# Four batches mixed at once in the quarters of the matmul array, with four row buffers

## The chip, the cores and the metric

The kernel runs on one core of a Trainium2 chip. The metric is the time of one execution on the device in microseconds; smaller is better. Several runs of a kernel are given as their median.

## What is computed

A batch of 32 inputs of 64 channels by 1024 positions passes through two layers. Cut to what matters:

```python
# layer 0: grouped convolution + condition, then an FFN with 4-bit weights and low-rank parts
x = x + ffn0(conv(x, cond))
# layer 1: every batch b has a mixing matrix of its own, then one of 8 experts for each row
agg_w = einsum('bk,koi->boi', att, weight)            # att: softmax of a small MLP of cond
agg_b = att @ bias_k
z = einsum('boi,bih->boh', agg_w, x) + agg_b[:, :, None]   # 32 x 64 rows of 1024
logits = z.reshape(2048, 1024) @ gate_w.T + gate_b
selected = argmax(softmax(logits))
x = x + z_row @ expert_w[selected].T + expert_b[selected]
```

The change touches the line that makes `z`, and the logits and the row numbers behind it.

## The kernel before

The 2048 rows (32 batches of 64 channels) lie in SBUF as 16 row tiles `acc[:, t]` of 128 partitions by 1024 FP32 values, 4 KB in each partition. Tile `t` holds batch 2t in partitions 0 to 63 and batch 2t + 1 in partitions 64 to 127. Each engine runs its own program; the programs meet only at semaphores. The matmul unit (TensorE, PE in the profile) writes to eight PSUM banks of 128 x 512 FP32; two banks side by side are a `pair`.

Layer 0 fills some 1065 us and ends when VectorE (DVE) has added the last product to `acc` (semaphore `acc_added`, 352 counts). While its last products run, SyncE (SP) stores the finished rows to DRAM (`x_rows`, line 408), and the mixing matrices are made and written to DRAM (`batch_kernels`, line 481, issued by GpSimd, POOL) and read back (line 486).

The *mixing loop* follows, over the 16 row tiles, with these steps for tile `t`:

- `z_product` (line 1323): the block-diagonal matrix `bdg[:, t]`, 128 x 128 with the two batches' 64 x 64 matrices on its diagonal and zeros elsewhere, times `acc[:, t]`. Two FP32 matmuls of 512 columns, into pair 0 for even tiles and pair 2 for odd ones. A `memset` on GpSimd (line 478) made the zeros.
- `z_bias` (line 718): ScalarE (ACT) adds the mixed bias and writes the 128 x 1024 result to `z32[:, t % 2]`, one of two buffers. It waits for the product, for the store that last read this buffer (`z_stored`), and for the transposes that last read it.
- line 499: GpSimd issues the store of the buffer to DRAM (`z_rows`), from where the expert stage gathers rows later.
- `z_transposed` (line 1331): TensorE turns the buffer in eight 128 x 128 transposes into pair 1.
- `z_copied` (line 989): VectorE copies all of pair 1 into the one SBUF tile `zt`.
- `gate` (line 1339): eight narrow FP32 matmuls, on four strips of 32 columns of the array, give the 8 experts' logits in four parts; `logit` (line 996) adds the gate bias; `pick_out` (line 1346) sums the parts with one small matmul, and `picked` (line 1001) copies the 8 logits of each row to `logits`.

TensorE's order is: transposes of tile t, product of tile t + 2, gate of t, pick of t - 1. VectorE's is: copy of t, logit of t, picked of t - 1. SyncE loads the weights of experts 0 and 1 (`wraw`, line 425, 512 KB each time), one load after each tile's activation.

Then comes routing: VectorE finds each row's expert and slot, a matmul of one-hot matrices gives the table from slots to row numbers (lines 1037 to 1079), and TensorE turns dummy products (`spin`, line 1369) meanwhile. A row number is built from two digits: the lane (`lane`, partition + 1) and the tile number times 128. The expert stage then gathers rows of `z_rows` by that table (line 518), transposes them and multiplies, up to the end.

Of the kernel before, what the change touches and what calls it, by code (L numbers as in the profile page):

```python
# [9 lines left out]
I32 = mybir.dt.int32  # L10
# [35 lines left out]
ONEHOT = 5  # L46
EMPTY = 1 << 20
# [39 lines left out]
def program(nc, x_nat, x_conv, toep, cond_t, ctx_w_t, chan_bias, codes_up, codes_dn, am_up, am_dn, bias_up,  # L87
# [5 lines left out]
    with ctx:  # L93
# [60 lines left out]
        wh = sb(late, "wh", [P, 2, 4, L], F32R)  # L154
        hh = sb(late, "hh", [P, 4, CHUNK], F32R)
# [10 lines left out]
        sb(tail, "gts_too", [P, KT, GQ])  # L166
# [37 lines left out]
        lane = sb(moe, "lane", [P, 1])  # L204
        before = sb(moe, "before", [P, E, E])
# [46 lines left out]
        agg_mm, agg_ready, aggs_stored, bdg_zero = sem("agg_mm"), sem("agg_ready"), sem("aggs_stored"), sem("bdg_zero")  # L252
# [17 lines left out]
        bdg_in = sem("bdg_in")  # L270
# [4 lines left out]
        z_stored = [sem(f"z_stored{i}") for i in range(2)]  # L275
# [30 lines left out]
        def _(sp):  # L306
# [104 lines left out]
            sp.wait_ge(bdg_zero, 1)  # L411
# [27 lines left out]
        def _(pool):  # L439
# [37 lines left out]
            pool.wait_ge(term_ready, NCH * WT)  # L477
            nc.gpsimd.memset(bdg[:], 0.0).then_inc(bdg_zero, 1)
# [11 lines left out]
            nc.gpsimd.iota(lane_i[:], [[1, 1]], base=1, channel_multiplier=1).then_inc(iotas, 1)  # L490
            nc.gpsimd.memset(tri[:], 1.0).then_inc(iotas, 1)
            pool.wait_ge(iotas, 3)
# [3 lines left out]
            for i in rounds(pool, TILES // 2):  # L496
                for k in range(2):
                    wait(pool, z_ready, i * 2 + k + 1)
                    pool.dma_start(z_dram[bass.ds(i * 2 * P + k * P, P)], z32[:, k]).then_inc(z_stored[k], 16)

            for k in range(2):
                pool.wait_ge(z_stored[k], 16 * TILES // 2)
                pool.wait_ge(x_stored[k], 16 * TILES // 2)
# [65 lines left out]
        def _(act):  # L569
# [144 lines left out]
            def z_bias(i, p):  # L714
                act.wait_ge(z_mm, i * 2 + p + 1)
                wait(act, z_stored[p % 2], i * 16 + 16 * (p // 2))
                wait(act, z_tr, i * 2 + p - 1)
                nc.scalar.activation(z32[:, p % 2], pair[2 * (p % 2)][:], ACT.Identity,  # L718
                                     bias=aggb[:, bass.ds(i * 2 + p, 1)]).then_inc(z_ready, 1)

            z_bias(0, 0)
            z_bias(0, 1)
            for i in rounds(act, TILES // 2 - 1):
                for k in range(2):
                    z_bias(i, k + 2)
# [30 lines left out]
        def _(dve):  # L756
            def perceptron(step):
# [15 lines left out]
                else:  # L773
                    dve.wait_ge(aggb_mm, 1)
                    for c in range(2):
                        rows = slice(64 * c, 64 * c + 64)
                        nc.vector.tensor_copy(aggb[rows, :], bank[3][rows, 0:B].rearrange(
                            "p (q c) -> p q c", c=2)[:, :, c]).then_inc(aggb_ready, 1)
# [207 lines left out]
            def z_copied(i, k):  # L986
                dve.wait_ge(z_tr, i * 2 + k + 1)
                wait(dve, gate_mm, i * 2 + k)
                nc.vector.tensor_copy(zt[:], pair[1][:]).then_inc(zt_ready, 1)

            def logit(i, k):
                dve.wait_ge(gate_mm, i * 2 + k + 1)
                dve.sem_inc(dve_passed, 1)

                wait(dve, pick_mm, i * 2 + k - 1)
                nc.vector.tensor_scalar(lt[:, k], bank[6 + k][:, 0:P], gbs[:, 0:1], None, ALU.add).then_inc(lt_ready, 1)

            def picked(i, k):
                dve.wait_ge(pick_mm, i * 2 + k + 1)
                dve.sem_inc(dve_passed, 1)  # L1000
                nc.vector.tensor_copy(logits[:, bass.ds(i * 2 + k, 1)].rearrange("p t e -> p (t e)"),
                                      bank[6 + k][:, P:P + E]).then_inc(logit_ready, 1)

            for i in rounds(dve, TILES // 2):
                for k in range(2):
                    z_copied(i, k)
                    logit(i, k)
                    if k:
                        picked(i, 0)
                    elif not isinstance(i, int):  # L1010
                        picked(i - 1, 1)
                if isinstance(i, int):
                    dve.wait_ge(iotas, 4)
                    nc.vector.tensor_copy(lane[:], lane_i[:]).then_inc(route_const, 1)
                    nc.vector.tensor_copy(iota_f[:], iota_i[:]).then_inc(route_const, 1)
                    dve.wait_ge(route_const, 2)
                    nc.vector.tensor_scalar(rising[:], iota_f[:, 0:E], -1.0, float(E), ALU.mult, ALU.add).then_inc(route_const, 1)
                    nc.vector.tensor_scalar(room[:], iota_f[:, 0:TILES], float(ST), None, ALU.mult).then_inc(route_const, 1)
                    nc.vector.tensor_tensor(before[:], by_entry(iota_f[:, 0:E], E),
                                            iota_f[:, 0:E].rearrange("p (o e) -> p o e", o=1).broadcast_to([P, E, E]),  # L1020
                                            ALU.is_gt).then_inc(route_const, 1)
                    nc.vector.tensor_copy(tri_b[:], tri[:]).then_inc(route_const, 1)
                    nc.vector.tensor_copy(ones_b[:], ones[:]).then_inc(route_const, 1)
                    nc.vector.tensor_copy(iota_b[:], iota_f[:]).then_inc(route_const, 1)
                    dve.wait_ge(route_const, 8)
            picked(TILES // 2 - 1, 1)
# [39 lines left out]
            nc.vector.tensor_tensor(atcol[:, :, 1], attile[:], by_entry(iota_f[:, 0:TILES], SC), ALU.mult).then_inc(digits_ready, 1)  # L1066
# [10 lines left out]
            link(nc.vector.scalar_tensor_tensor(out=upper[:], in0=bank[3][:, SC:2 * SC], scalar=float(P), in1=empty[:],  # L1077
# [50 lines left out]
        def _(pe):  # L1128
# [190 lines left out]
            def z_product(i, p):  # L1319
                wait(pe, z_ready, i * 2 + p - 1)  # L1320
# [6 lines left out]
            def z_transposed(i, p):  # L1327
                pe.wait_ge(z_ready, i * 2 + p + 1)
                wait(pe, zt_ready, i * 2 + p)
                for kt in range(KT):  # L1330
                    ins = nc.tensor.transpose(pair[1][:, kt * P:(kt + 1) * P], z32[:, p % 2, kt * P:(kt + 1) * P], ident[:])
                ins.then_inc(z_tr, 1)

            def gate(i, p):
                pe.wait_ge(zt_ready, i * 2 + p + 1)
                wait(pe, lt_ready, i * 2 + p - 1)

                for kt in range(KT):
                    ins = mm(bank[6 + p][kt % 4 * GQ:(kt % 4 + 1) * GQ, 0:P], gts[:, kt], zt[:, kt * P:(kt + 1) * P],
                             start=kt < 4, stop=kt >= 4)  # L1340
                ins.then_inc(gate_mm, 1)

            def pick_out(i, k):
                pe.wait_ge(lt_ready, i * 2 + k + 1)
                wait(pe, logit_ready, i * 2 + k - 1)
                mm(bank[6 + k][:, P:P + E], lt[:, k], pick[:], start=True, stop=True).then_inc(pick_mm, 1)

            pe.wait_ge(gts_in, 32)
            pe.wait_ge(bdg_in, 32)
            pe.wait_ge(acc_added, TILES * (UNITS - 1) + 1)  # L1350
            z_product(0, 0)
            pe.wait_ge(acc_added, TILES * UNITS)
            z_product(0, 1)
            for i in range(TILES // 2):
                for k in range(2):
                    z_transposed(i, k)
                    if i < TILES // 2 - 1:
                        z_product(i, k + 2)
# [134 lines left out]
```

## Time and profile before

| | us |
|---|---|
| Median of 3 runs | 1441.71 (1440.62 to 1446.35) |
| Profiled execution, span from first to last instruction | 1438.6 |
| Layer 0, up to the last addition to `acc` | 0 to 1064.85 |
| Mixing loop, first product to last logits | 1064.96 to 1126.91 |
| Routing, up to the first gather | to 1140.2 |
| Expert stage | to the end |

The profile is of one execution. A row of the timeline gives the start of a group of equal instructions, the time from its first start to its last end, the engine, the line, the operation, what is written and read, and in square brackets how long the engine had been idle and what ended that. An FP32 matmul shows as two instructions. Matmuls are pipelined: the next one starts before the last one's end, so the step from start to start tells their pace and the duration does not.

### The profile page before, as it was taken

Reading aid. Unit: us, or ns where it says so; the run is one execution under the profiler, and the core shown is the slowest. Engines: PE = TensorE matmul, PEld = TensorE weight load, DVE = VectorE, ACT = ScalarE, POOL = GpSimd, SP = SyncE. Lnnn points to the kernel's source line nnn. Section 1 sums busy time; section 2 is a strip of 40 time slices with the busy share of each in tenths; the row PEclk is TensorE's granted clock in tenths of the full one; section 3 lists DMA queues with packets and bytes.
Section 4 is the critical chain, followed back from the end, with each engine's and each line's share of the span. In section 5 each row is a group of like instructions: output and inputs, shape, how many; then the busy total and the mean of one; then the engine's idle time right before and its main releaser. Section 6 shows DMA issues by size and latency. Waiting matters only on the chain.

```text
span 1438.6 us, 20752 instructions
## 1 busy us (share of the span) xinstructions
PE 1398.8 (97%) x6817; PEld 1146.1 (80%) x6817; DVE 1137.8 (79%) x1101; ACT 755.7 (53%) x839; POOL 211.0 (15%) x218
## 2 busy tenths in 40 slices
PE   7899999999999999999999999999999899999996
PEld 7888888888888888888888888887755688888785
DVE  6869887878877787887878878787644699999895
ACT  5655554545546455464554644643123277777672
POOL 0111000000000000000000000000011266665443
PEclk9999999999999999999999999999999999999998
DMA  6864656568665686656865667756668547969951
GB/s 221 315 223 165 236 209 254 196 250 273 237 246 203 234 292 229 227 218 227 294 240 206 240 220 281 256 191 240 238 231 287 160 121 194 354 190 303 332 146 35
DMA packets 102680, 331.48 MB, mean 230 GB/s; under 512 B 15220, under 2 KB 22908, under 8 KB 102620
## 3 DMA queue, kind: packets, MB, share of 16 engines
q1 hardware_dynamic: 79556, 258.56, 48.4%
q0 software_dynamic: 22816, 71.85, 17.9%
q8 instruction: 30, 0.49, 0.1%
q10 hardware_dynamic: 256, 0.40, 0.1%
q14 instruction: 22, 0.18, 0.0%
HBM read 295.63 MB, written 46.14 MB: 238 GB/s over the span
## 4 chain that ended last, share of the span: by engine, by line
PE 85%; DMA 6%; DVE 3%; issue 2%; ACT 2%; SPq 0%; ACTq 0%; POOL 0%; DVEq 0%; POOLq 0%
PE pair L1133 26%; PE pair L1135 26%; PE pair L1134 25%; PE pair L1187 4%; DMA z_rows<-z 3%; DMA wraw<-exp_w 3%; PE pair L1402 1%; DVE wf L808 1%; PE pair L1214 1%; PE pair L1271 1%; PE pair L1197 1%; ACT z L718 1%; DVE wlr L1108 1%; PE pair L1369 1%; PE pair L1183 1%
## 5 line engine op out<-in xcount | busy, mean ns | idle before, releaser
L808 DVE TENSOR_TENSOR wf<-wf,term 128x1024 f32<-128x1024 f32 x308 | 376.7, 1223 | 65.7 <-ACT term L593 50.5
L593 ACT ACTIVATE term<-codes 128x1024 f32<-128x1024 int32 x308 | 320.6, 1054 | 139.4 <-DVE wf L808 139.4
L1133 PE MATMUL pair<-wh,hh 128*128 128x512 f32 x672 | 263.4, 392 | 3.2 <-DVE ring L871 1.4
L1134 PE MATMUL pair<-wl,hh 128*128 128x512 f32 x672 | 262.0, 390 | 0.0
L1135 PE MATMUL pair<-wh,hl 128*128 128x512 f32 x672 | 262.0, 390 | 0.0
L1133 PE MATMUL pair<-ring,wh 128*128 128x512 f32 x656 | 255.5, 390 | 0.0
L1134 PE MATMUL pair<-ring,wh 128*128 128x512 f32 x656 | 255.3, 389 | 0.0
L1135 PE MATMUL pair<-ring,wl 128*128 128x512 f32 x656 | 255.2, 389 | 0.0
L741 ACT ACTIVATE whr<-wraw 128x1024 fp32r x184 | 187.9, 1055 | 85.3 <-PE pair L1135 50.8
L866 DVE TENSOR_TENSOR acc<-acc,pair 128x1024 f32<-128x1024 f32 x160 | 194.4, 1216 | 47.2 <-PE pair L1135 39.8
L1108 DVE TENSOR_TENSOR wlr<-wraw,whr 128x1024 fp32r<-128x1024 f32 x184 | 213.3, 1215 | 12.5 <-ACT whr L741 12.2
L1133 PEld LDWEIGHTS pair<-wh,hh 128*128 128x128 f32 x672 | 126.2, 188 | 34.3 <-DVE acc L866 3.0
L1133 PE MATMUL pair<-whr,zth 128*128 128x512 f32 x368 | 146.4, 398 | 4.8 <-DVE ztl L1096 4.8
L1135 PEld LDWEIGHTS pair<-wh,hl 128*128 128x128 f32 x672 | 126.1, 188 | 26.5
L1134 PEld LDWEIGHTS pair<-wl,hh 128*128 128x128 f32 x672 | 126.3, 188 | 25.9
L1135 PE MATMUL pair<-whr,ztl 128*128 128x512 f32 x368 | 144.2, 392 | 0.0
L1134 PE MATMUL pair<-wlr,zth 128*128 128x512 f32 x368 | 144.0, 391 | 0.0
L1135 PEld LDWEIGHTS pair<-ring,wl 128*128 128x128 f32 x656 | 123.2, 188 | 25.7
L1133 PEld LDWEIGHTS pair<-ring,wh 128*128 128x128 f32 x656 | 123.2, 188 | 25.3
L1134 PEld LDWEIGHTS pair<-ring,wh 128*128 128x128 f32 x656 | 123.2, 188 | 25.1
L622 ACT ACTIVATE wh<-wf 128x1024 fp32r<-128x1024 f32 x44 | 45.6, 1058 | 177.6 <-DVE wf L827 162.8
L473 POOL DMA_DIRECT2D acc<-x_nat x16 | 13.9, 870 | 771.1 <-DVE acc L866 771.1
(178 smaller groups left out, 1527.6 us busy)
## 6 DMA issues: line engine op xcount, KB each, us to landing
ring<-x_parts SPq DMA_DIRECT2D x320, 512.0 KB, 6.4
wraw<-exp_w SPq DMA_DIRECT2D x64, 512.0 KB, 11.2
x_parts<-stage POOLq DMA_DIRECT2D x24, 512.0 KB, 6.0
xg<-exp_b POOLq DMA_DIRECT2D x23, 512.0 KB, 8.0
codes<-codes_up SPq DMA_DIRECT2D x22, 512.0 KB, 5.8
codes<-codes_dn SPq DMA_DIRECT2D x22, 512.0 KB, 5.6
am<-am_dn SPq DMA_DIRECT2D x22, 512.0 KB, 3.7
acc<-x_nat POOLq DMA_DIRECT2D x16, 512.0 KB, 5.5
```

The lines of the kernel that those rows point to most:

```text
L593: return nc.scalar.activation(out, codes[:, n % 2], ACT.Relu, scale=scale, bias=-scale * bend)
L622: nc.scalar.activation(high_part(n), whole(n), ACT.Copy).then_inc(wh_ready, 1)
L718: nc.scalar.activation(z32[:, p % 2], pair[2 * (p % 2)][:], ACT.Identity, bias=aggb[:, bass.ds(i * 2 + p, 1)]).then_inc(z_ready, 1)
L741: nc.scalar.activation(whr[:, kt], wraw[:, bass.ds(buf, 1), kt].rearrange("p a n -> p (a n)"), ACT.Copy).then_inc(whr_ready, 1)
L808: nc.vector.tensor_tensor(whole(n), whole(n), term[:, e % 2], op).then_inc(term_added, 1)
L866: nc.vector.tensor_tensor(a, a, pair[2 + j % 2][:], ALU.add).then_inc(acc_added, 1)
L1108: nc.vector.tensor_tensor(wlr[:, kt], wraw[:, bass.ds(buf, 1), kt].rearrange("p a n -> p (a n)"), whr[:, kt], ALU.subtract).then_inc(wlr_r ...
L1133: mm(ps, ah, bh, start=first, stop=False)
L1134: mm(ps, ah, bl, start=False, stop=False)
L1135: return mm(ps, al, bh, start=False, stop=last)
L1183: mm(whole_bank, ones[:].bitcast(F32R), ctxd[h][:, k - LATE * h:k - LATE * h + 1].broadcast_to([P, J, CH]), start=True, stop=False)
L1187: ins = mm(whole_bank[:, :, g * GC:(g + 1) * GC], xcv[h][p % 4][:, k % 2, g, d:d + P], tz[h][:, d, g], start=False, stop=g == GROUPS - 1 a ...
```

## The change

- A product takes two row tiles, `2u` and `2u + 1`, with four batches. Each batch's 64 x 64 matrix is used alone: `aggw` holds them without zeros. For each half of the columns, four matmuls of 64 rows by 64 columns go to the four quarters of the array. The row half of the array is the half of the tile that is read (`half`), the column half is the tile (`c`).
- So the results lie in another order: new tile `t = 2u + s` holds batch 4u + s in partitions 0 to 63 and batch 4u + 2 + s in partitions 64 to 127. Each buffer is therefore stored with two transfers of 64 partitions, and the slot table, its constants `lane` and `tile_f`, and the bias `aggb` hold the new order.
- `z32` has four buffers, laid over `hh` and `hl`. `zt` has two, and pair 1 is transposed and copied in two halves of 512 columns. Gate and picks run one tile later, in another order.
- The memset of `bdg` goes. What waited for it waits for the end of the 4-bit weights' conversion. The weight loads of experts 0 and 1 wait for other counts. The loops on ScalarE, VectorE and GpSimd are written out.

```diff
+        z32 = sb(mix, "z32", [P, 4, L])
-        z32 = sb(dyn, "z32", [P, 2, L])
-        bdg = sb(dyn, "bdg", [P, TILES, P])
+        aggw = sb(dyn, "aggw", [P, TILES, CH])
-        zt = sb(dyn, "zt", [P, L])
+        zt = sb(dyn, "zt", [P, 2, L])
...
-                        sp.wait_ge(z_ready, KT * e + kt + 1)
+                        sp.wait_ge(z_ready, TILES if e else 2 * kt + 1)
                     sp.dma_start(wraw[:, e % 2, kt], exp_w[e, :, kt]).then_inc(wraw_in[e % 2][kt], 16)
...
-            nc.gpsimd.memset(bdg[:], 0.0).then_inc(bdg_zero, 1)
...
-            pool.wait_ge(bdg_zero, 1)
+            pool.wait_ge(term_ready, NCH * WT)
+            pool.wait_ge(term_added, NCH * WT)
             pool.wait_ge(aggs_stored, 64)
             for c in range(2):
-                pool.dma_start(bdg[c * CH:(c + 1) * CH, :, c * CH:(c + 1) * CH], bd_dram.rearrange(
-                    "(t c) i o -> c i t o", c=2)[c]).then_inc(bdg_in, 16)
+                pool.dma_start(aggw[c * CH:(c + 1) * CH], bd_dram.rearrange("(t c) i o -> c i t o", c=2)[c]).then_inc(aggw_in, 16)
...
-            for i in rounds(pool, TILES // 2):
-                for k in range(2):
-                    wait(pool, z_ready, i * 2 + k + 1)
-                    pool.dma_start(z_dram[bass.ds(i * 2 * P + k * P, P)], z32[:, k]).then_inc(z_stored[k], 16)
+            z_rows = z_dram.rearrange("(u c s o) l -> u s c o l", c=2, s=2, o=CH)
+            for t in range(TILES):
+                pool.wait_ge(z_ready, t + 1)
+                for c in range(2):
+                    pool.dma_start(z_rows[t // 2, t % 2, c], z32[c * CH:(c + 1) * CH, t % 4]).then_inc(z_stored[t % 4], 16)
...
+            def z_bias(t):
+                act.wait_ge(z_mm, t // 2 + 1)
+                wait(act, z_stored[t % 4], 32 * (t // 4))
+                wait(act, z_tr, 2 * (t - 3))
+                nc.scalar.activation(z32[:, t % 4], pair[2 * (t % 2)][:], ACT.Identity, bias=aggb[:, t:t + 1]).then_inc(z_ready, 1)
...
+            def z_copied(t):
+                for h in range(2):
+                    dve.wait_ge(z_tr, 2 * t + h + 1)
+                    wait(dve, gate_mm, t - 1)
+                    nc.vector.tensor_copy(zt[:, t % 2, h * 512:(h + 1) * 512], bank[2 + h]).then_inc(zt_ready, 1)
...
+                nc.vector.tensor_copy(tile_f[:], tile_i[:]).then_inc(route_const, 1)
+                nc.vector.tensor_scalar(lane[CH:P], lane[CH:P], float(CH), None, ALU.add).then_inc(route_const, 1)
...
+            for u in range(TILES // 2):
+                z_copied(2 * u)
+                if u:
+                    picked(2 * u - 2)
+                    logit(2 * u - 1)
+                z_copied(2 * u + 1)
+                if u:
+                    picked(2 * u - 1)
+                logit(2 * u)
+                if u == 0:
+                    constants()
...
-            nc.vector.tensor_tensor(atcol[:, :, 1], attile[:], by_entry(iota_f[:, 0:TILES], SC), ALU.mult).then_inc(digits_ready, 1)
+            nc.vector.tensor_tensor(atcol[:, :, 1], attile[:], by_entry(tile_f[:], SC), ALU.mult).then_inc(digits_ready, 1)
...
+            def z_product(u):
+                wait(pe, z_ready, 2 * u)
                 for h in range(2):
-                    rows = acc[:, i * 2 + p, h * 512:(h + 1) * 512]
-                    ins = mm(bank[4 * (p % 2) + h], bdg[:, i * 2 + p], rows,
-                             start=True, stop=True)
+                    d = slice(h * 512, (h + 1) * 512)
+                    for c in range(2):
+                        for half in range(2):
+                            rows = slice(half * CH, (half + 1) * CH)
+                            ins = mm(bank[4 * half + h][c * CH:(c + 1) * CH], aggw[rows, 2 * u + c], acc[rows, 2 * u + c, d],
+                                     start=True, stop=True)
                 ins.then_inc(z_mm, 1)
+            def z_transposed(t):
+                pe.wait_ge(z_ready, t + 1)
+                for h in range(2):
+                    wait(pe, zt_ready, 2 * t + h - 1)
+                    for kt in range(4 * h, 4 * h + 4):
+                        ins = nc.tensor.transpose(bank[2 + h][:, kt % 4 * P:(kt % 4 + 1) * P],
+                                                  z32[:, t % 4, kt * P:(kt + 1) * P], ident[:])
+                    ins.then_inc(z_tr, 1)
...
+            pe.wait_ge(aggw_in, 32)
+            pe.wait_ge(acc_added, TILES * UNITS - 1)
+            z_product(0)
             pe.wait_ge(acc_added, TILES * UNITS)
+            for u in range(TILES // 2):
+                z_transposed(2 * u)
+                if u:
+                    pick_out(2 * u - 2)
+                    gate(2 * u - 1)
+                if u < TILES // 2 - 1:
+                    z_product(u + 1)
+                z_transposed(2 * u + 1)
+                if u:
+                    pick_out(2 * u - 1)
+                gate(2 * u)
```

## Rows read from the trace of the kernel before

**Rows 1.** Timeline, stage start: start, duration, engine, line, what [idle before, releaser].
```profile
1063.63 1.22 DVE L866 TENSOR_TENSOR acc<-acc,pair 128x1024 f32<-128x1024 f32 x1 [1.05 <-PE pair L1135]
1064.96 3.67 PE L1323 MATMUL pair<-acc,bdg 128*128 128x512 f32 x8 [1.36 <-issue]
1067.01 1.11 ACT L718 ACTIVATE z<-pair,aggb 128x1024 f32<-128x1024 f32 x1 [14.30 <-PE pair L1323]
```

**Rows 2.** Timeline, stage end: the last tile's transposes, store issue and logits.
```profile
1122.56 1.09 PE L1331 MATMUL pair<-ident,z 128*128 128x128 f32 x8 [0.23 <-ACT z L718]
1123.17 0.53 POOL L499 DMA_DIRECT2D z_rows<-z  x1 [3.94 <-ACT z L718]
...
1126.74 0.17 DVE L1001 COPY logits<-pair 128x8 f32<-128x8 f32 x1 [0.40 <-PE pair L1346]
```

**Rows 3.** Chain of waits near the stage's end: start, us, what.
```profile
1115.27 5.97 DMA z_rows<-z
1121.39 1.12 ACT z L718
```

**Rows 4.** Windows: PE, PEld, DVE, ACT, POOL busy (instructions), clock, DMA share, GB/s.
```profile
1095.00:1105.00 10.00, 10.00 (x87) 5.70 (x86) 4.96 (x8) 3.34 (x3) 1.29 (x3) 1.00 0.94 306
1105.00:1115.00 10.00, 10.00 (x87) 5.87 (x86) 4.96 (x9) 3.34 (x3) 1.59 (x3) 1.00 0.88 299
...
1127.00:1140.00 13.00, 12.28 (x87) 10.26 (x86) 10.09 (x47) 0.00 (x0) 0.00 (x0) 1.00 0.01 3
```

**Rows 5.** Waits, 1064 to 1127 us: who waited for whom, total, times, longest.
```profile
ACT z L718 <- DMA z_rows<-z: 32.2, 12, 4.4
...
PE pair L1331 <- ACT z L718: 0.9, 2, 0.6
```

**Rows 6.** Timeline of one tile in the steady part, TensorE and VectorE.
```profile
1111.91 1.07 PE L1331 MATMUL pair<-ident,z 128*128 128x128 f32 x8
1111.92 0.35 DVE L996 TENSOR_SCALAR lt<-pair,gbs 128x128 f32<-128x128 f32 x1 [1.21 <-PE pair L1339]
...
1112.82 1.88 PE L1323 MATMUL pair<-acc,bdg 128*128 128x512 f32 x4
1113.02 1.23 DVE L989 COPY zt<-pair 128x1024 f32<-128x1024 f32 x1 [0.56 <-PE pair L1331]
...
1114.63 0.65 PE L1339 MATMUL pair<-zt,gts 128*32 128x128 f32 x16
...
1115.20 0.39 PE L1346 MATMUL pair<-pick,lt 128*128 128x8 f32 x2
...
1115.45 0.41 PE L1331 MATMUL pair<-ident,z 128*128 128x128 f32 x2
```

**Rows 7.** All transposes: ns min/median/max, first and last start in us.
```profile
L1331 PE MATMUL pair<-ident,z x128: 272/273/329, 1068.5 to 1123.4; 128*128 128x128 f32 x128
```

**Rows 8.** All products of the mixing loop, in the same form.
```profile
L1323 PE MATMUL pair<-acc,bdg x64: 592/592/667, 1065.0 to 1117.6; 128*128 128x512 f32 x64
```

**Rows 9.** Timeline: matmuls on four column strips, and on two row halves.
```profile
1047.50 1.06 PE L1170 MATMUL pair<-kerns,att_t 8*32 8x512 f32 x8
...
1056.16 0.40 PE L1271 MATMUL pair<-wl,hh 64*128 64x512 f32 x2
1056.40 0.39 PE L1271 MATMUL pair<-wh,hl 64*128 64x512 f32 x2
```

**Rows 10.** Groups of equal shape: a 512-column VectorE read of PSUM, count, busy, mean.
```profile
L871 DVE TENSOR_TENSOR stage<-pair,stage 128x512 fp32r<-128x512 f32 x24 | 16.5, 689 | 9.3 <-ACT stage L638 9.1
```

**Rows 11.** Timeline: the first and the last of eight routing constants on VectorE.
```profile
1075.67 0.14 DVE L1014 CAST lane<-lane_i 128x1 f32<-128x1 int32 x1
...
1076.55 0.22 DVE L1024 CAST iota_b<-iota_f 128x128 bf16<-128x128 f32 x1
```

**Rows 12.** The sixteen z stores (line 499): issue to landing.
```profile
DMA to landing us min/median/max: 4.4/5.1/7.3
```

**Rows 13.** Chain of waits: the first gather of the expert stage.
```profile
1140.23 4.33 DMA zg<-z_rows,table
```

More of the change, by code:

```diff
@@ L46 @@
 ONEHOT = 5
+CONSTS = 10
 EMPTY = 1 << 20
@@ L274, in program @@
         gts_in, digits_ready = sem("gts_in"), sem("digits_ready")
-        z_stored = [sem(f"z_stored{i}") for i in range(2)]
+        z_stored = [sem(f"z_stored{i}") for i in range(4)]
         x_stored = [sem(f"x_stored{i}") for i in range(2)]
@@ L712, in _ @@
             act.wait_ge(aggb_ready, 2)
[L714 to L725, printed above, removed]
+            def z_bias(t):
[3 more added lines that the diff above has]
+                nc.scalar.activation(z32[:, t % 4], pair[2 * (t % 2)][:], ACT.Identity, bias=aggb[:, t:t + 1]).then_inc(z_ready, 1)
+            for t in range(TILES):
+                z_bias(t)
             def z_high(i, s):
@@ L776, in perceptron @@
                         rows = slice(64 * c, 64 * c + 64)
-                        nc.vector.tensor_copy(aggb[rows, :], bank[3][rows, 0:B].rearrange(
-                            "p (q c) -> p q c", c=2)[:, :, c]).then_inc(aggb_ready, 1)
+                        nc.vector.tensor_copy(aggb[rows, :].rearrange("p (u s) -> p u s", s=2), bank[3][rows, 0:B].rearrange(
+                            "p (u c s) -> p u c s", c=2, s=2)[:, :, c]).then_inc(aggb_ready, 1)
             dve.wait_ge(ident_ready, 2)
@@ L984, in by_entry @@
                 return column.rearrange("p (t o) -> p t o", o=1).broadcast_to([P, column.shape[1], entries])
[L986 to L1025, printed above, removed]
@@ L1026, in _, with logit @@
-            picked(TILES // 2 - 1, 1)
+            def z_copied(t):
[3 more added lines that the diff above has]
+                    nc.vector.tensor_copy(zt[:, t % 2, h * 512:(h + 1) * 512], bank[2 + h]).then_inc(zt_ready, 1)
+            def logit(t):
+                dve.wait_ge(gate_mm, t + 1)
+                wait(dve, pick_mm, t - 1)
+                nc.vector.tensor_scalar(lt[:, t % 2], bank[6 + t % 2][:, 0:P], gbs[:, 0:1], None, ALU.add).then_inc(lt_ready, 1)
@@ new lines, in picked, with constants @@
+            def picked(t):
+                dve.wait_ge(pick_mm, t + 1)
+                nc.vector.tensor_copy(logits[:, t], bank[6 + t % 2][:, P:P + E]).then_inc(logit_ready, 1)
+            def constants():
+                dve.wait_ge(iotas, 5)
+                nc.vector.tensor_copy(lane[:], lane_i[:]).then_inc(route_const, 1)
+                nc.vector.tensor_copy(iota_f[:], iota_i[:]).then_inc(route_const, 1)
+                nc.vector.tensor_copy(tile_f[:], tile_i[:]).then_inc(route_const, 1)
+                dve.wait_ge(route_const, 3)
+                nc.vector.tensor_scalar(lane[CH:P], lane[CH:P], float(CH), None, ALU.add).then_inc(route_const, 1)
+                nc.vector.tensor_scalar(rising[:], iota_f[:, 0:E], -1.0, float(E), ALU.mult, ALU.add).then_inc(route_const, 1)
+                nc.vector.tensor_scalar(room[:], iota_f[:, 0:TILES], float(ST), None, ALU.mult).then_inc(route_const, 1)
+                nc.vector.tensor_tensor(before[:], by_entry(iota_f[:, 0:E], E),
+                                        iota_f[:, 0:E].rearrange("p (o e) -> p o e", o=1).broadcast_to([P, E, E]),
+                                        ALU.is_gt).then_inc(route_const, 1)
+                nc.vector.tensor_copy(tri_b[:], tri[:]).then_inc(route_const, 1)
+                nc.vector.tensor_copy(ones_b[:], ones[:]).then_inc(route_const, 1)
+                nc.vector.tensor_copy(iota_b[:], iota_f[:]).then_inc(route_const, 1)
+                dve.wait_ge(route_const, CONSTS)
@@ L1027, in _ @@
+            for u in range(TILES // 2):
[9 more added lines that the diff above has]
+                    constants()
+            picked(TILES - 2)
+            logit(TILES - 1)
+            picked(TILES - 1)
             step = [0]
@@ L1076, in _ @@
             link(nc.vector.tensor_scalar(empty[:], bank[3][:, 0:SC], 0.0, float(EMPTY), ALU.is_equal, ALU.mult))
-            link(nc.vector.scalar_tensor_tensor(out=upper[:], in0=bank[3][:, SC:2 * SC], scalar=float(P), in1=empty[:],
+            link(nc.vector.scalar_tensor_tensor(out=upper[:], in0=bank[3][:, SC:2 * SC], scalar=float(CH), in1=empty[:],
                                                 op0=ALU.mult, op1=ALU.add))
@@ L1334, in gate @@
[L1334 to L1339, printed above, removed]
+                    d = slice(h * 512, (h + 1) * 512)
[4 more added lines that the diff above has]
+                                     start=True, stop=True)
@@ L1340, in gate, with pick_out @@
+            def gate(t):
+                pe.wait_ge(zt_ready, 2 * t + 2)
+                wait(pe, lt_ready, t - 1)
+                for kt in range(KT):
+                    ins = mm(bank[6 + t % 2][kt % 4 * GQ:(kt % 4 + 1) * GQ, 0:P], gts[:, kt], zt[:, t % 2, kt * P:(kt + 1) * P],
                              start=kt < 4, stop=kt >= 4)
                 ins.then_inc(gate_mm, 1)
[L1343 to L1346, printed above, removed]
+            def pick_out(t):
+                pe.wait_ge(lt_ready, t + 1)
+                wait(pe, logit_ready, t - 1)
+                mm(bank[6 + t % 2][:, P:P + E], lt[:, t % 2], pick[:], start=True, stop=True).then_inc(pick_mm, 1)
@@ L1348, in _ @@
             pe.wait_ge(gts_in, 32)
-            pe.wait_ge(bdg_in, 32)
-            pe.wait_ge(acc_added, TILES * (UNITS - 1) + 1)
-            z_product(0, 0)
+            pe.wait_ge(aggw_in, 32)
+            pe.wait_ge(acc_added, TILES * UNITS - 1)
+            z_product(0)
             pe.wait_ge(acc_added, TILES * UNITS)
[L1353 to L1358, printed above, removed]
-                    gate(i, k)
-                    if k:
-                        pick_out(i, 0)
-                    elif i > 0:
-                        pick_out(i - 1, 1)
@@ L1364, in _ @@
-            pick_out(TILES // 2 - 1, 1)
+            for u in range(TILES // 2):
[9 more added lines that the diff above has]
+                gate(2 * u)
+            pick_out(TILES - 2)
+            gate(TILES - 1)
+            pick_out(TILES - 1)
```

28 lines of the change are left out of this document (13 added, 15 removed).

## The prediction

> **What bounds the kernel now.** I read the stage windows first, since the change touches one stage only: the mixing loop, from its first product at 1064.96 us [rows 1] to the last logits at 1126.91 us, ahead of the first routing step [rows 2], 61.95 us. The chain of waits names the engine at the end of each step, and in this loop it shows z stores and the z activation behind them [rows 3]. Read alone it says that the two z buffers are the bound. The windows say otherwise: TensorE is busy 10.00 of 10.00 us in the two from 1095 to 1115 us [rows 4]. The table of waits settles it: ScalarE waited 32.2 us for stores in 12 places, but TensorE waited only 0.9 us in 2 places for ScalarE [rows 5]. So the stores are late by almost as much as TensorE needs; TensorE sets the pace, and the stores add the few gaps. One tile in the steady part [rows 6]: the transposes start at 1111.91, the product at 1112.82, the gate matmuls at 1114.63, the pick at 1115.20, the next tile's transposes at 1115.45. That is 0.91 + 1.81 + 0.57 + 0.25 = 3.54 us, half of it the product. The sixteen groups of transposes start from 1068.5 us on [rows 7], the last at 1122.56 [rows 2]: 54.1 / 15 = 3.61 us per tile, near the 3.54.
>
> The profiled execution's span is 1438.6 us, the median of the runs 1441.71. I take 3.1 us as lying around the span and unchanged, and apply the difference to both.
>
> **The products.** One product is two 128x512 FP32 matmuls, which show as four instructions with starts (1.88 - 0.59) / 3 = 0.43 us apart [rows 6, 8]: a pair of tiles now holds 2 x 1.81 = 3.62 us. The change gives a pair eight 64x64 matmuls, sixteen instructions of 512 columns each. If the four quarters run side by side these are four rounds of 0.43, and with the same 0.09 to the next kind of matmul (1.81 - 4 x 0.43) 1.82 us. Two rows say that narrow matmuls overlap. The aggregation's eight instructions on four column strips take 1.06 us in all [rows 9], where one after the other they would take 0.60 + 7 x 0.43 = 3.6: two rounds of four. The gate's sixteen take 0.65 us, four rounds of four with different moving data for each strip [rows 6]. The last down products on two row halves go in twos, 0.24 us apart [rows 9], the pace of one. No row has both halvings at once. Lower bound: 1.82, as each quarter must stream 4 x 512 columns. Upper bounds: two at a time, eight rounds, 3.53 us; one at a time, sixteen rounds, 6.97 us. I take 1.82, since strips of either kind overlap fully in the rows nearest to it.
>
> **The rest of TensorE's pair.** Transposes, gate and pick keep their counts: 2 x (0.91 + 0.57 + 0.25) = 3.46. Pair: 3.46 + 1.82 = 5.28 us against 7.08, or 7.22 at the pace with gaps.
>
> **What could be late next.** VectorE: the 1.23 us copy becomes two of 512 columns, 0.69 each by the nearest row [rows 10]; with 0.35 and 0.17 for logits [rows 2, 6] that is 1.90 us a tile, 3.80 a pair, under 5.28. The first half-copy starts while the second four transposes run, so the gate one step later finds its tile ready. The pick waits for logits queued behind a second half-copy: at most 0.15 us a pair. ScalarE: 2 x 1.11 a pair. GpSimd queue: four store issues of 0.53 [rows 2], 2.1 us a pair; the register steps of the loops go. The routing constants (eight instructions, the first at 1075.67 and the last ending at 1076.77 [rows 11], and now two more, some 1.5 us) still sit on VectorE after the first pair; VectorE's spare 1.48 a pair absorbs most, I charge 0.5 once.
>
> **The stores.** Four buffers instead of two: a buffer is needed again two pairs after its activation, 2 x 5.3 - 1.1 = 9.5 us after that ended. The store is issued 0.66 us after the end (1122.51 to 1123.17 [rows 2, 3]), the second half 0.53 later, and landing took 4.4 to 7.3 us [rows 12]: 5.6 to 8.5. It fits with 1.0 us to spare at the slowest. The bytes: a tile moves 512 KB of z out and 512 KB of expert weights in per 3.54 us now, 296 GB/s; the new gates on the weight loads (two activations per load of expert 0, all of expert 1 after the last) make it three times 512 KB per pair of 5.3 us, again 297. The DMA engines were 0.94 busy at 306 GB/s [rows 4], so about 306 / 0.94 = 326 is the limit and this fits. Expert 1's eight loads, 4.2 MB, take 13 us at that rate from about 1106 us on and end by about 1121; the first gather [rows 13], now at 1140.2, comes at 1125. They fall into a stretch that had 3 GB/s [rows 4]. Cost 0; if they ran over, the gather's 4.33 us [rows 13] would grow by at most the same again.
>
> **Half-height stores.** Each store is now two transfers of 64 partitions. No row shows a 4 KB-per-partition transfer of half height. Bounds: nothing (not below, as the bytes are the same and the issues more), or each half as long as a whole, 4.4 us more at least [rows 12], by which the slowest would be 8.5 + 4.4 - 9.5 = 3.4 us late. I take 0, by the whole stores' landing times, which move the same bytes through the same queue, and keep the other end as a rival. The Trainium skill speaks against this edit ("SBUF — State Buffer", Door 1: The DMA port swizzle): partitions 0 to 63 reach 8 of the 16 ports, and 64 partitions gave 196 GB/s where 128 gave 328. No run here shows it yet.
>
> **Edges.** Both weight transfers behind the first product are 256-byte pieces as before, issued behind the same aggregation; the removed memset and the waits put in its place end at about 982 us, long before. The last accumulation ends at 1064.85 [rows 1]; the first product may wait for the one before it, so cost 0. It does both tiles in 1.82, where two products took 3.5: the first activation starts at 1067.0 as now, the transposes at 1068.1 instead of 1068.5. First pair, without picks: 0.91 + 0.2 for the second activation + 1.82 + 0.91 + 0.57 = 4.4, to 1072.5. Six pairs of 5.31 and 0.5 for constants: 1104.9. The last pair has no product: its last transposes start 0.91 + 0.25 + 0.57 later, 1106.6. From there to the last logits now took 1126.91 - 1122.56 = 4.35 [rows 2]; add 0.15 for the second half-copy and 0.5 for logit steps that now stand between: 1111.6, up to 1112 with hops. Gain 61.95 - 46.9 = 15 us. The slot table costs the same: its new row numbers are two small VectorE operations off the path. The expert stage starts 15 us earlier and is paced by its own products.
>
> Forecast: 1438.6 - 15 = 1423.6 us of span, 1441.7 - 15 = **1427 us**.
>
> **Rivals.** *Two quarters at a time.* Pair 3.46 + 3.53 = 6.99 against 7.22: the gain is some 1.7 us, 1440. For it: no row with both halvings; against it: each overlaps alone. *Stores somewhat late.* Landing of 9 to 11 us would make a buffer late every second pair and take back 2.5 to 9 us: 1429.5 to 1436. For it: stores already land at up to 7.3 with the DMA engines 0.9 busy. The price is 0.7 to 2.7 us each, three or four times over the loop. *Half-height stores at half rate, which hold up the loads too.* A pair then asks for five units of 512 KB at 326 GB/s, 8.05 us instead of 5.31: 2.74 x 6 gives back 16.4 us, to 1443, no gain. The skill's port rule taken at its worst is this case. Against it: the stores' share of the bytes is 2 in 3 and their rate alone, 1.05 MB per 5.3 us = 198 GB/s, has not been seen to block loads. *One quarter after another*, the slower end: 6.97 us, pair 10.4, eight times 5.15 more than forecast: 1427 + 41 = 1468. It decides from a product of about 3.7 us on, where 8 x (3.7 - 1.82) eats the gain. Against it: the rows of narrow matmuls. That the quarters do not run together at all is also the case in which the change does not do what it says.
>
> **How the numbers follow.** Forecast (1424 to 1430) 0.58; stores somewhat late 0.16; two at a time 0.09; half rate 0.09; one after another 0.08. The first two and two-at-a-time fill the range from 1424 to 1441, 0.83. A measurement of this kernel tells about 0.5% from no change, 7.2 us: faster is below 1434.5. That holds the forecast and most of the late stores, 0.72; same, 1434.5 to 1449, the rest of these, two at a time and half rate, 0.20; slower 0.08.
>
> **What would show it.** Right: sixteen product instructions of a pair within about 1.9 us, starting in fours; transposes of even tiles some 5.3 us apart; ScalarE waits for products, hardly for stores; the last logits near 1112 us; routing of 12 to 13 us after it, as now. Wrong: eight or sixteen separate rounds; z landings over 9 us with ScalarE waiting for them and TensorE for ScalarE; granted clock below 1.00 in the stage, which no window of before shows [rows 4]; or a first gather that waits for expert 1's loads.

## The result and the profile after

The changed kernel took 1423.84 us in the median of four runs (1421.99 to 1431.12), the one before 1441.85, also in four: ratio 0.9875, 95% interval 0.9845 to 0.9904. It is faster by 18.0 us, where 15 were forecast. The forecast was 1427.0 in a range from 1424 to 1441; the median lies 0.16 us below the range.

The mechanism went as forecast. One pair of tiles in the steady part of the mixing loop, TensorE alone, in the timeline of the kernel after (start, us, line, what):

```profile
1097.42 1.95 PE L1333 MATMUL pair<-acc,aggw 64*64 64x512 f32 x16
...
1099.29 1.09 PE L1342 MATMUL pair<-ident,z 128*128 128x128 f32 x8
...
1100.22 0.29 PE L1358 MATMUL pair<-pick,lt 128*128 128x8 f32 x2
1100.44 0.64 PE L1351 MATMUL pair<-zt,gts 128*32 128x128 f32 x16
...
1101.02 1.09 PE L1342 MATMUL pair<-ident,z 128*128 128x128 f32 x8
...
1101.94 0.29 PE L1358 MATMUL pair<-pick,lt 128*128 128x8 f32 x2
1102.16 0.64 PE L1351 MATMUL pair<-zt,gts 128*32 128x128 f32 x16
1102.74 1.95 PE L1333 MATMUL pair<-acc,aggw 64*64 64x512 f32 x16
```

From product to product 5.32 us (5.31 forecast), the product 1.87 of it (1.82 forecast). In [rows 6] one tile alone took 3.54, half of it the product. Narrow windows on the same product show the rounds: four instructions start within 0.02 us, four more 0.48 us later, the next four 0.43 us after those:

```profile
1097.42 0.66 PE L1333 MATMUL pair<-acc,aggw 64*64 64x512 f32 x4
1097.90 1.04 PE L1333 MATMUL pair<-acc,aggw 64*64 64x512 f32 x8
1098.33 1.04 PE L1333 MATMUL pair<-acc,aggw 64*64 64x512 f32 x8
```

(The second and third rows hold that round and the next.) The waits in the loop, where [rows 5] had ScalarE waiting 32.2 us for stores (engine, line, waited for, total us, times, longest), and the z stores' issue to landing, the answer to [rows 12]:

```profile
ACT z L724 <- PE pair L1333: 35.0, 8, 13.7
POOL z_rows L504 <- ACT z L724: 23.3, 8, 3.2
...
PE pair L1342 <- ACT z L724: 1.4, 1, 1.4
DMA to landing us min/median/max: 4.3/5.2/8.6
```

ScalarE now waits for products alone; no wait for a store is left. The longest landing, 8.6 us, is that of the last store of all, whose buffer is not needed again; of the stores before the last tile's none took over 6.9 us. The ends of the loop, to be read beside [rows 1, 2], and the first gather, beside [rows 13]:

```profile
1065.87 1.22 DVE L868 TENSOR_TENSOR acc<-acc,pair 128x1024 f32<-128x1024 f32 x1 [1.04 <-PE pair L1142]
1066.62 1.95 PE L1333 MATMUL pair<-acc,aggw 64*64 64x512 f32 x16 [0.78 <-issue]
...
1074.41 1.10 PE L1342 MATMUL pair<-ident,z 128*128 128x128 f32 x8
1079.74 1.09 PE L1342 MATMUL pair<-ident,z 128*128 128x128 f32 x8
...
1108.06 1.09 PE L1342 MATMUL pair<-ident,z 128*128 128x128 f32 x8
1112.29 0.17 DVE L1001 COPY logits<-pair 128x8 f32<-128x8 f32 x1 [0.48 <-PE pair L1358]
1125.55 4.35 DMA zg<-z_rows,table
```

Read in this way from each profile (end of the last accumulation, end of the last logits copy, start of the first gather, end of the span), the stages are, in us:

| kernel | layer 0 | mixing loop | routing | gather to end | span |
|---|---|---|---|---|---|
| before | 1064.86 | 62.06 | 13.32 | 298.34 | 1438.58 |
| before, again | 1067.68 | 62.31 | 13.33 | 300.05 | 1443.37 |
| after | 1067.09 | 45.36 | 13.10 | 297.18 | 1422.73 |
| after, again | 1065.72 | 45.68 | 13.09 | 298.03 | 1422.52 |
| after, third | 1064.99 | 45.34 | 13.07 | 303.20 | 1426.61 |

The loop gave 16.6 us (62.06 less 45.46, the mean of the three profiles after), routing 0.2. Layer 0 and the expert stage move by some us from one execution to the next, in both kernels.

### The profile page after: what moved, and what is told of

Its sections match the earlier page's. It is cut to its first block, busy times and chain, and to the rows that moved or that the text cites. A ratio compares the mean times of both kernels' runs of the same rounds, so it can differ in the third digit from the quotient of the medians.

```text
span 1422.7 us, 20751 instructions
## 1 busy us (share of the span) xinstructions
PE 1385.2 (97%) x6881; PEld 1141.3 (80%) x6881; DVE 1136.3 (80%) x1119; ACT 754.9 (53%) x839; POOL 213.2 (15%) x234
## 4 chain that ended last, share of the span: by engine, by line
PE 91%; DVE 3%; DMA 2%; issue 1%; ACT 1%; ACTq 0%; SPq 0%; DVEq 0%; POOL 0%; POOLq 0%
PE pair L1140 27%; PE pair L1141 26%; PE pair L1142 26%; PE pair L1194 4%; PE pair L1416 1%; PE pair L1342 1%; PE pair L1333 1%; DVE wf L810 1%; DMA wraw<-exp_w 1%; PE pair L1221 1%; PE pair L1278 1%; PE pair L1204 1%; PE pair L1351 1%; PE pair L1383 1%; DVE wlr L1115 1%
## 5 line engine op out<-in xcount | busy, mean ns | idle before, releaser
L478 POOL DMA_DIRECT2D acc<-x_nat x16 | 13.7, 859 | 771.2 <-DVE acc L868 749.6
```

## The experiments

Two things had to be told apart: what made the gain (quarters, buffers, or both), and why the gain by medians was larger than the loop's. The code edits are cut to what matters; `...` marks a cut.

**The changed kernel again** (no edit, label after_again).

> The changed kernel once more, in more rounds, to size the step that was missed. The profiled execution has a span of 1422.7 us against 1438.6, 15.9 us less, while the medians differ by 18.0. If the 2 us between them is scatter of layer 0, where nothing changed and the profiled execution reached its last addition 2.2 us later than before, the ratio comes nearer to 0.989 (gain 15.5 to 17). If something outside the mixing loop also became faster for good, it stays at 0.9875 (gain 18) or below. Pair of tiles in the mixing loop: 5.32 us in both cases.

Measured: 1423.55 us, ratio 0.9868 (0.9844 to 0.9891), loop 45.68 us. That fits a steady gain better than scatter, so the question stayed open for further runs.

**Block-diagonal products in the changed kernel** (blocks).

```diff
-                        for half in range(2):
...
-                            ins = mm(bank[4 * half + h][c * CH:(c + 1) * CH], aggw[rows, 2 * u + c], acc[rows, 2 * u + c, d],
...
+                        ins = mm(bank[4 * c + h], bdg[:, 2 * u + c], acc[:, 2 * u + c, d], start=True, stop=True)
```

The memset, the slot table's constants and the row order go back with it.

> The changed kernel with block-diagonal 128x128 products again, in the old row order: four buffers, half copies, half-height stores and the order of the steps stay. Theory (TensorE was the bound, the quarters are the gain): a product of a pair takes 3.53 us again, a pair 5.32 + 1.71 = 7.0 us against 7.22 before, the time is 1 to 2 us under that of before, ratio 0.9985 to 1.0. Rival (the two buffers and the stores behind them were the bound, as the chain of waits of before says): most of the gain stays, ratio under 0.992, pair under 6 us.

Measured: 1440.81 us, ratio 0.9988 (0.9969 to 1.0007), loop 58.85 us. Product and transposes of one pair, and the transposes of the next pair:

```profile
1086.15 3.70 PE L1334 MATMUL pair<-acc,bdg 128*128 128x512 f32 x8
1089.69 1.04 PE L1342 MATMUL pair<-ident,z 128*128 128x128 f32 x8
...
1096.61 1.04 PE L1342 MATMUL pair<-ident,z 128*128 128x128 f32 x8
```

A pair takes 6.92 us with a product of 3.54. All that the change brings besides the quarters is worth 3.2 us in the loop, somewhat more than expected; how the four buffers, the half copies and the new order of the steps share in it was not tried. The rival that the chain of waits in [rows 3] suggests, the buffers as the only bound, falls.

**Two z buffers in the changed kernel** (two_buffers).

```diff
-        z32 = sb(mix, "z32", [P, 4, L])
+        z32 = sb(mix, "z32", [P, 2, L])
-                wait(act, z_stored[t % 4], 32 * (t // 4))
-                wait(act, z_tr, 2 * (t - 3))
+                wait(act, z_stored[t % 2], 32 * (t // 2))
+                wait(act, z_tr, 2 * (t - 1))
...
```

Wherever the buffer's number was `t % 4`, it is `t % 2`.

> The changed kernel with two z buffers instead of four, all else as it is. Theory: an activation now waits for the store of the tile two before it, so a pair takes the activation 1.11, the issue 0.66 + 0.53, a landing of 4.3 to 8.6 and the second activation, 7.7 us or more against 5.32; over seven pairs at least 17 us more, the time is that of before or above (ratio to before 0.998 to 1.01). Rival (quarters alone suffice): within 3 us of the changed kernel, ratio 0.988 to 0.990.

Measured: 1440.01 us, ratio 0.9993 (0.9975 to 1.0012), loop 59.79 us, 14.3 more than with four. In its table of waits the stores are back, and now TensorE waits behind them:

```profile
ACT z L723 <- DMA z_rows<-z: 29.9, 6, 5.9
...
PE pair L1341 <- ACT z L723: 11.6, 7, 3.4
```

These waits of TensorE come to 11.6 us, where the changed kernel has 1.4: 10.2 of the 14.3 us. Part of the rest can be the clock: behind waits of 3.4 and 2.1 us, TensorE ran two stretches of this loop at a granted clock of 0.50 (1.2 GHz), where every window of the changed kernel's loop has 1.00 (columns as in [rows 4]):

```profile
1077.40:1080.80 3.40, 3.40 (x30) 2.96 (x34) 1.60 (x4) 1.11 (x1) 2.09 (x4) 0.50 0.71 176
1108.10:1111.50 3.40, 3.40 (x26) 0.80 (x16) 0.76 (x3) 0.00 (x0) 0.95 (x2) 0.50 0.89 349
```

So the change without its quarters takes 3.2 us off the loop, and without its two further buffers 2.3. In the kernel before, the stores were late by almost as much as TensorE needed; only with both loosened does the loop get much shorter.

**Each quarter product twice** (product_twice).

```diff
-                for h in range(2):
+                for h in (0, 1, 0, 1):
```

> The changed kernel, but each quarter product is made twice into the same place, so the result stays. Theory (TensorE still sets the pace of a pair): four more rounds of 0.43 us in each of eight products, 8 x 1.72 = 13.7 us more than the changed kernel, pair 7.04 us, ratio to before 0.997. Rival (after the change the stores or the DMA engines at 0.94 set the pace, and TensorE has slack): under 5 us more, ratio below 0.992.

Measured: loop 59.49 us against 45.46 in the mean of the three profiles of the changed kernel, 14.0 more (13.7 expected), pair 7.04 us. TensorE has no slack after the change either. The time, 1443.03 us, is 3 us above that sum (1426.0, the mean of all runs of the changed kernel, and 14.0); in its profile the expert stage took 303.0 us.

**The kernel before again** (no edit, before_again).

> The kernel before against itself, for a second profile of it. The gain of the change by the medians (18.0 and 19.5 us in two sets of runs) is larger than what the mixing loop and routing gave between the profiles (62.06 - 45.5 and 13.3 - 13.1, 16.8 us). Scatter of the expert stage: ratio within 0.998 to 1.002, and in this profile the stretch from first to last expert product is not 277.0 us again but anything from 275 to 281, as in the kernels with changed loops. Steady gain of the expert stage by the change: 277 to 281 here against 275 to 276 in every profile of the changed kernel.

Measured: ratio 0.9989 (0.997 to 1.0008); expert products 278.7 us from first to last. Inside both bands, so it does not decide alone.

**The changed kernel a third time** (after_third).

> The changed kernel a third time, beside the one before on the same chip. Mixing loop from the last accumulation to the last logits 45.4 to 45.7 us as in the two other profiles. If the expert stage only scatters, its products take anything from 275 to 281 us and the ratio comes to 0.988 to 0.9895; if it gained for good, 275 to 276 and 0.9865 to 0.988.

Measured: 1428.98 us, ratio 0.9905 (0.9876 to 0.9934), loop 45.34 us, expert products 281.0 us. Scatter: the same kernel had 275.1 and 275.9 in its other two profiles. The ratio lies above both bands: the three sets of runs scatter too, with 0.9875, 0.9868 and 0.9905. All runs together, 16 of the changed kernel and 80 of the one before, have means of 1426.0 and 1442.3 us, 16.2 apart; the loop and routing gave 16.8 between the profiles.

**Stores of 128 partitions** (whole_store).

```diff
-                for c in range(2):
-                    pool.dma_start(z_rows[t // 2, t % 2, c], z32[c * CH:(c + 1) * CH, t % 4]).then_inc(z_stored[t % 4], 16)
+                pool.dma_start(z_dram[t * P:(t + 1) * P], z32[:, t % 4]).then_inc(z_stored[t % 4], 16)
...
```

The counts that wait for a store, 32 for each buffer, become 16.

> The changed kernel with each z buffer stored by one transfer of 128 partitions, into rows in the buffers' order; the gather by the old table then reads other rows, so the output is not that of the reference. Theory (half-height stores cost nothing here, four buffers cover them): time within 0.2% of the changed kernel, landing 4.4 to 7.5 us instead of 4.3 to 8.6, pair 5.32. Rival (half-height stores keep the DMA engines busier and hold up the weight loads): 2 us or more faster.

Measured: 1431.49 us, ratio 0.9922 (0.9892 to 0.9952), loop 45.78 us. Their landing:

```profile
DMA to landing us min/median/max: 5.7/6.5/8.9
```

No gain from whole stores: the loop is the same within 0.3 us, and the time is not below the changed kernel's. The landing missed its band of 4.4 to 7.5 us. The row cannot be set beside the 4.3/5.2/8.6 of the halves, which carry half the bytes, and of which the two of a buffer count on one semaphore. The buffer is free when its second half has landed, and in the trace of the changed kernel that is 6.5 us after the first half's issue in the median of the sixteen buffers: the same as the 6.5 here.

**Neighbours in the program share a quarter** (quarter_by_quarter).

```diff
-                for h in range(2):
-                    for c in range(2):
-                        for half in range(2):
+                for c in range(2):
+                    for half in range(2):
...
+                        for h in range(2):
...
```

> The changed kernel, but a quarter's two column halves are issued one right after the other, so neighbours in the program share a quarter. Theory (matmuls start in program order, and one that waits for its own quarter holds back those behind it): quarters overlap only at their seams, a product takes 3.5 to 5.7 us instead of 1.87, the time is 13 to 31 us more than the changed kernel, ratio to before 0.997 to 1.01. Rival (each quarter takes its own work in order, past a waiting neighbour): 1.9 us, no change, ratio 0.987.

Measured: 1427.74 us, ratio 0.9898 (0.9863 to 0.9932), loop 46.05 us. The theory failed, the rival was right:

```profile
1096.96 1.97 PE L1333 MATMUL pair<-acc,aggw 64*64 64x512 f32 x16
1098.86 1.09 PE L1342 MATMUL pair<-ident,z 128*128 128x128 f32 x8
```

```profile
1096.96 0.68 PE L1333 MATMUL pair<-acc,aggw 64*64 64x512 f32 x4
1097.44 1.06 PE L1333 MATMUL pair<-acc,aggw 64*64 64x512 f32 x8
```

A product takes 1.90 us in that order too, again in rounds of four (second fence, narrow windows on the same product; its second row holds two rounds). The order in which the program names the quarters does not matter here.

**Light weights, before and after** (before_light, after_light; the same edit in both).

```diff
-                    sp.dma_start(wraw[:, e % 2, kt], exp_w[e, :, kt]).then_inc(wraw_in[e % 2][kt], 16)
+                    n = L if e < 2 else L // 4
+                    sp.dma_start(wraw[:, e % 2, kt, 0:n], exp_w[e, :, kt, 0:n]).then_inc(wraw_in[e % 2][kt], 16)
```

> The kernel before with a quarter of the columns of the weights of experts 2 to 7 loaded (the rest of each buffer keeps an earlier expert's, so the output is not that of the reference; all products stay). Theory (the scatter between executions is the expert stage waiting for weight loads that land late, and the half clock behind such waits): expert products 271 to 273 us instead of 277 to 279, runs within 2 us of each other instead of 10, median 1434 to 1438. Rival (the scatter sits in layer 0 or in the clock by itself): runs spread over 6 us or more as before.

> The changed kernel with the same weights left out (experts 2 to 7, three quarters of the columns; the output is not that of the reference). Theory: the difference from the light kernel before is the mixing loop and routing alone, 16.5 to 17 us by the medians, with expert products 271 to 273 us in both. Rival (the change also makes the expert stage shorter for good): 18 us or more.

Measured: 1436.4 (1432.9 to 1440.4) and 1418.79 us (1416.5 to 1422.3), 17.6 apart, between the two expected values; by means 1436.4 and 1419.2, 17.1 apart. Expert products 271.7 and 270.1 us. The two profiles differ by less, 15.2 us of span: their loops are 60.70 and 45.66 us, 15.0 apart. So the loop of the kernel before also moves, from 60.70 to 62.31 us in its three profiles, and the gain read from a pair of profiles with it. ScalarE's waits for weights, in the third profile of the changed kernel and in the two light ones, after first and before second:

```profile
ACT whr L743 <- DMA wraw<-exp_w: 14.3, 11, 3.5
```

```profile
ACT whr L744 <- DMA wraw<-exp_w: 0.7, 2, 0.4
```

```profile
ACT whr L742 <- DMA wraw<-exp_w: 0.6, 2, 0.3
```

With light loads these waits are nearly gone, and the kernel before took 1436.4 instead of 1442.86 us. But the runs still spread over 6 to 8 us, so late weights are one source of the scatter and not all of it. Another shows in the profiles: the first accumulation starts anywhere from 201.2 to 204.2 us, and from there to the end of the last one it is 863.7 us in each of the five profiles in the table. It goes with the granted clock near 60 us, here in the kernel before and before again (columns as in [rows 4]):

```profile
55.00:70.00 15.00, 11.87 (x45) 9.58 (x46) 13.05 (x12) 8.37 (x10) 1.84 (x4) 0.89 0.59 234
55.00:70.00 15.00, 11.32 (x43) 9.10 (x42) 14.01 (x14) 7.86 (x9) 2.10 (x4) 0.77 0.66 252
```

Where this window has 0.89 (before, after again, after third) the first accumulation starts at 201.2, 202.0 and 201.3 us; where it has 0.77 (before again, after) at 204.0 and 203.4. Whether the clock is the cause was not tried.

**Half a product** (half_product).

```diff
-                for h in range(2):
+                for h in range(1):
```

> The changed kernel with the second 512 columns of each product left out (the activation reads whatever is in those banks, so the output is not that of the reference). If TensorE still sets the pace at a shorter pair: 8 x 0.86 = 6.9 us less in the mixing loop, pair 4.46. If what is next late, the stores behind four buffers (2 x 4.46 - 1.11 = 7.8 us of cover for 1.2 us of issue and landings of 4.3 to 8.6): 2 to 5 us less, ScalarE waits for stores.

Measured: 1415.24 us, ratio 0.9813 (0.9787 to 0.9838), loop 39.09 us, 6.4 less than 45.46. One pair:

```profile
1087.45 1.09 PE L1342 MATMUL pair<-ident,z 128*128 128x128 f32 x8
...
1089.18 1.09 PE L1342 MATMUL pair<-ident,z 128*128 128x128 f32 x8
...
1091.92 1.09 PE L1342 MATMUL pair<-ident,z 128*128 128x128 f32 x8
```

4.47 us, with no wait for a store in its table. TensorE would still be the bound with a product half as long.

**Transposes copied whole** (whole_copy).

```diff
-                for h in range(2):
-                    dve.wait_ge(z_tr, 2 * t + h + 1)
...
-                    nc.vector.tensor_copy(zt[:, t % 2, h * 512:(h + 1) * 512], bank[2 + h]).then_inc(zt_ready, 1)
+                dve.wait_ge(z_tr, 2 * t + 2)
...
+                nc.vector.tensor_copy(zt[:, t % 2], pair[1][:]).then_inc(zt_ready, 2)
```

> The changed kernel with the transposes copied whole, one copy of 1024 columns for each tile, as before. The next tile's transposes then wait for the whole copy (1.23 us and the hops), which ends while the pick, the gate and the product run where a product stands between, and delays them where none does: by 0.1 to 0.6 us a pair, mixing loop 46 to 50 us instead of 45.5, ratio within 0.003 of the changed kernel. Theory of the prediction (VectorE has slack in every pair): at the lower end.

Measured: 1431.2 us, ratio 0.9936 (0.9906 to 0.9965), loop 53.48 us, 8.0 more. The second transposes of a pair come 2.56 us after the first instead of 1.73, and their own row names the copy:

```profile
1085.85 1.09 PE L1341 MATMUL pair<-ident,z 128*128 128x128 f32 x8
...
1087.04 1.22 DVE L991 COPY zt<-pair 128x1024 f32<-128x1024 f32 x1 [2.04 <-issue]
...
1088.41 1.06 PE L1341 MATMUL pair<-ident,z 128*128 128x128 f32 x8 [0.76 <-DVE zt L991]
1091.97 1.09 PE L1341 MATMUL pair<-ident,z 128*128 128x128 f32 x8
```

The expectation failed: 0.8 us in every pair, above its upper end. The copy starts 1.19 us after the transposes and takes 1.22; the next transposes wait for it, and pick and gate, which take 0.80 us of TensorE's time between the two, do not cover it. Half copies let the first bank go while the second is being filled. They are a third piece, without which 8.0 of the 16.6 us are lost.

## Why the prediction was right and wrong

- *The bound.* Right: TensorE set the pace, although the chain of waits named stores. blocks and product_twice show it, each from its own side.
- *Quarters side by side, 1.82 us.* Right: 1.87, four at once; the extra 0.05 is the first step of 0.48 us where 0.43 was taken. No row of before had both halvings at once, and the value at the nearest rows held.
- *Pair of 5.28 to 5.31 us.* Right: 5.32.
- *Stores behind four buffers, half height at no cost.* Right: landing 4.3 to 8.6 against 4.4 to 7.3 [rows 12], and no wait. What the Trainium skill states ("SBUF — State Buffer", Door 1: The DMA port swizzle), 196 GB/s for 64 partitions where 128 gave 328, no run here shows, as no store of this loop runs without other transfers beside it. No loss is seen in the loop: 6.5 us for two halves of 256 KB and for one whole store (whole_store).
- *Half copies.* The prediction entered them under what could be late, at a cost of at most 0.15 us a pair, and not as part of the gain. whole_copy shows that 8.0 us of it hang on them.
- *DMA limit of 326 GB/s.* Wrong, without effect: dividing 306 by a busy share of 0.94 [rows 4] is no limit. The third profile of the changed kernel moved 417 GB/s in one window (below). Expert 1's loads did fit: routing took 13.1 us, and the first gather 4.35 against 4.33 [rows 13].
- *The loop's sum, 15 us.* This is the step that failed, by size: under "Edges" the sum lets the loop after end 47.0 us after the last accumulation, and it took 45.46 (45.34 to 45.68), so that the gain is 16.6 us (15.0 between the light kernels, whose loop before was shorter). Three of its terms were too large. The 0.5 for constants cost nothing: the transposes of pairs one and two start 5.33 us apart, 1074.41 and 1079.74. From the last transposes to the last logits I added 0.65 and more to the 4.35 of before; it is 4.40, since the steps that came between fit beside others. The first product started 0.47 us before the last accumulation ended (1066.62 and 1067.09), where I let it start with it; its transposes start 2.85 us after that end (1069.94), 3.25 were summed.
- *3.1 us around the span.* Wrong: the profiled execution after has 1424.34 us for a span of 1422.7, 1.6 around it, and before_again 1444.87 for 1443.4. So the profile of before was not of a median execution but of a faster one. Only differences were used, and nothing else hangs on it.
- *The range.* Its lower end stood 3 us under the forecast and held the bounds of the costs alone. The runs shown of the kernel before already spread by 5.7 us, and the median of four scatters with them. The 1.5 us missed in the loop, 0.2 in routing, 1.2 us of scatter (18.0 less 16.8) and the 0.3 by which the sum's 1426.7 had been rounded up to 1427 make the 3.2 us between forecast and median, 0.16 more than the range allowed. On which side of the end a median falls is luck: the third set of runs has 1428.98. Against the mean of all runs, 1426.0 us, the forecast is 1.0 off.
- *Expert stage unchanged.* Not refuted: 297.2 to 303.2 us after, 298.3 and 300.1 before, and 0.7 us between the two light kernels. A gain of 1 us or so could hide in the scatter.

## What to carry to other kernels

When two limits lie within a few per cent of each other, loosening one shows next to nothing: here the change without its quarters left the loop at 58.85 us (6.92 us a pair) and without its two further buffers at 59.79 (6.2 to 8.0 us a pair), against 62.06 before and 45.46 with all, and the chain of waits names only one of the two. Ask whether the bounding engine ever waits (the waits table and the busy time in a window), not which wait is longest. Then take out one piece of a change at a time: the half copies, which looked like a detail, held half of the gain. And set a range by the spread of the runs as well as by the unknown costs.

## What was not expected of the hardware

- Quarters of the array keep their own order: with two products for one quarter next to each other in the program, the sixteen instructions still took 1.97 us, four at a time as when neighbours went to different quarters.
- Two stores of 64 partitions freed their buffer as soon as one of 128 in the same loop, 6.5 us after the first issue in the median.
- The DMA engines' busy share is no measure of what is left: 0.94 went with 306 GB/s in [rows 4], and in the third profile of the changed kernel a share of 1.03 with 417 GB/s.
- In the same window of the expert stage the granted clock is 0.50 (1.2 GHz) for 3.4 us, after TensorE had waited 2.12 us for `ztl`; in [rows 4] and in the loop after it is 1.00 (columns as in [rows 4]):

```profile
1236.00:1246.00 10.00, 7.88 (x32) 6.04 (x32) 10.00 (x10) 8.36 (x9) 4.87 (x6) 0.83 1.03 417
1240.90:1244.30 3.40, 3.40 (x9) 2.52 (x8) 3.40 (x5) 2.40 (x3) 1.86 (x2) 0.50 1.04 424
```

```profile
1239.91 0.49 PE L1140 MATMUL pair<-whr,zth 128*128 128x512 f32 x1 [2.12 <-DVE ztl L1103]
```
